# Pieces of an early key and value projection placed at the ends of two earlier stages of a decoder kernel

## The reference, cut to what matters

```python
x = layernorm(x + attention0(x))            # layer 0
x = layernorm(x + cross_attention0(x, ctx))
x3 = layernorm(x + quantised_ffn0(x))
xn = layernorm(x3)                          # layer 1
mx = silu(conv(xn, ema_kernel) + xn * omega)
x4 = layernorm(gated_attention(x3, xn, mx))
K = ctx @ Wk.T + bk                         # 16 heads of 64, L1_xattn
V = ctx @ Wv.T
...
out = mixture_of_experts(layernorm(x4 + cross_attention1(x4, K, V)))
```

## Time and profile before

| | |
|---|---|
| median of 3 runs | 2559.37 us (2551.48 to 2562.3) |
| profiled execution | 2562.5 us, span 2560.5 us |
| PE busy | 2319.6 us, 91% of the span |
| ACT, DVE, POOL busy | 45%, 53%, 33% |
| mean granted clock of TensorE | 0.962 of 2.4 GHz |
| the four stages end (first work of the next) at | 837.8, 982.5, 1144.8 us for l0_xattn, l0_ffn, mega_conv |

### The profile page before, as it was taken

One profiled execution on the slowest core, in us unless ns is written; L12 is line 12 of the kernel. 1 busy time (PEld: TensorE's weight loads), 2 busy tenths in 40 slices (PEclk: granted clock), 3 DMA queues, 4 the chain that ended last, 5 costly groups with the idle time before them and its releaser, 6 DMA issues. The chain is left out here.

```text
span 2560.5 us, 45165 instructions
## 1 busy us (share of the span) xinstructions
PE 2319.6 (91%) x17378; PEld 1806.3 (71%) x17378; DVE 1345.0 (53%) x2520; ACT 1147.0 (45%) x1965; POOL 844.7 (33%) x873
## 2 busy tenths in 40 slices
PE   6999998799997897989898969999998799999993
PEld 5677777466665565756565758888886688888893
DVE  5688888478877670003544446778877211111113
ACT  4567676356665563434323235555564111111113
POOL 4354554234444581000101023445544212121221
PEclk9899999799999898999999989999999899999997
DMA  3524544100110569362111022333332665666564
GB/s 108 127 76 123 138 128 118 56 28 26 51 50 26 192 225 267 133 213 90 51 49 50 14 110 83 121 116 100 104 98 96 257 194 175 196 175 196 170 222 143
DMA packets 212899, 313.25 MB, mean 122 GB/s; under 512 B 63824, under 2 KB 195536, under 8 KB 199376
## 3 DMA queue, kind: packets, MB, share of 16 engines
q1 hardware_dynamic: 190832, 255.25, 31.6%
q0 software_dynamic: 13440, 17.90, 3.9%
q10 hardware_dynamic: 8416, 37.23, 3.7%
HBM read 188.88 MB, written 121.45 MB: 121 GB/s over the span
## 5 line engine op out<-in xcount | busy, mean ns | idle before, releaser
L2773 ACT ACTIVATE dec_area<-me_ps_h 128x512 f32<-128x512 f32 (+1 forms) x160 | 88.7, 555 | 423.7 <-PE me_ps_h L2751 414.9
L2814 DVE TENSOR_SCALAR me_yo<-me_ps_y,moe_xg 128x256 f32<-128x256 f32 x72 | 34.8, 484 | 429.2 <-PE me_ps_y L2761 410.2
L2689 POOL DMA_INDIRECT xo<-me_yo,me_row x72 | 112.7, 1566 | 410.8 <-DVE me_yo L2814 357.3
L2751 PE MATMUL me_ps_h<-me_xt,me_w 128*128 128x256 f32 (+1 forms) x1056 | 210.0, 357 | 0.0
L2761 PE MATMUL me_ps_y<-me_w,dec_area 128*128 128x256 f32 x944 | 209.2, 379 | 0.7 <-DVE me_yo L2814 0.7
L2224 POOL TENSOR_TENSOR l1x_e<-l1x_e,l1x_ri 128x1024 f32<-128x1024 f32 x64 | 121.7, 1902 | 240.2 <-DVE l1x_ri L2484 240.2
L2761 PEld LDWEIGHTS me_ps_y<-me_w,dec_area 128*128 128x128 f32 x944 | 178.7, 190 | 25.1 <-issue 1.1
L2751 PEld LDWEIGHTS me_ps_h<-me_xt,me_w 128*128 128x128 f32 x1056 | 181.7, 190 | 20.2
L868 POOL TENSOR_TENSOR l0x_e<-l0x_e,l0x_ri 128x1024 f32<-128x1024 f32 x64 | 120.0, 1896 | 199.5 <-DVE l0x_ri L1088 199.5
L2323 PE MATMUL l1x_ps_p<-l1x_xct,dec_area 128*128 128x256 f32 x512 | 125.9, 391 | 0.7 <-ACT l1x_xct L2409 0.7
L2361 PE MATMUL l1x_ps_o<-dec_area,l1x_ot 128*128 128x256 f32 x512 | 120.4, 389 | 1.4 <-ACT l1x_ot L2432 1.4
(11 more groups left out here) (423 smaller groups left out, 5530.7 us busy)
## 6 DMA issues: line engine op xcount, KB each, us to landing
me_w<-in_w SPq DMA_DIRECT2D x33, 2048.0 KB, 9.4
xs<-dec_zero SPq DMA_DIRECT2D x31, 1032.0 KB, 6.8
k<-kv_kt ACTq DMA_DIRECT2D x16, 1024.0 KB, 4.2
v<-kv_va ACTq DMA_DIRECT2D x16, 1024.0 KB, 4.5
l1x_kt<-k SPq DMA_DIRECT2D x16, 1024.0 KB, 5.0
l1x_va<-v SPq DMA_DIRECT2D x16, 1024.0 KB
moe_w_first<-in_w SPq DMA_DIRECT2D x7, 2048.0 KB, 9.7
moe_xg<-xs SPq DMA_DIRECT2D x32, 258.0 KB, 2.9
```

The costliest lines, as they stand in the source:

```text
L2689: pool.indirect_dma_start(token_rows, bass.IndirectOffsetOnAxis(row[:, j % 2, q:q + 1], 0), yo[:, j % 2, q, :], None, compute_op=ALU.add). ...
L2751: last = pe.matmul(ps_h[i % HB][:, f % 2, 0:P * size(j)], weights(j)[:, FFN * c + f * P:FFN * c + f * P + P], xt[:, j % 2, c, 0:P * size(j ...
L2773: act.activation(h[:, j % 2, 2 * i:2 * i + 2, 0:P * size(j)], ps_h[i % HB][:, :, 0:P * size(j)], ACT.Gelu).then_inc(gelued, 1)
```

## The change

Pieces 0 to 4 move into `l0_xattn`, behind its last steps; 8 pieces more go behind the last step of `l0_ffn`; all piece numbers in `l0_ffn` and `mega_conv` shift accordingly, so that 27 instead of 40 are left behind the convolution. In `l0_xattn` the pieces use the two projection banks ps_p.

```diff
+L0X_LAST, FFN_FIRST, FFN_STEP, FFN_LAST = 5, 10, 7, 8
...
         ps_p = [kit.ps(f"ps_p{i}", [P, GP]) for i in range(2)]
+        kv.share_banks(ps_p)
...
+                def early(n):
+                    if n == 0:
+                        pe.wait_ge(v_biased, TILES)
+                    kv.make(pe, n, n + 1)
                 walk([(0, TILES, score), (2, TILES, transpose_e), at_part(0, transposes), at_part(1, project_q), at_part(2, project_k),
-                      at_part(3, project_v), (2, TILES, apply), (3, TILES, multiply)])
+                      at_part(3, project_v), (2, TILES, apply), (3, TILES, multiply), (TILES + 1, L0X_LAST, early)])
...
                 walk([(2, TILES, copy_et), at_part(0, copy_xct), at_part(1, bias_q), at_part(2, bias_k), (0, TILES, exponentials),
-                      (2, TILES, copy_ot), (8, TILES, normalise)])
+                      (2, TILES, copy_ot), (8, TILES, normalise), (TILES + 1, 2, lambda n: kv.keep(act, n, n + 1)),
+                      (TILES + 5, L0X_LAST - 2, lambda n: kv.keep(act, n + 2, n + 3))])
...
+    def share_banks(self, banks):
+
+        self.ps = banks
...
-FFN_FIRST, FFN_STEP = 10, 7
...
-                kv.keep(act, 0, 2)
+                kv.keep(act, L0X_LAST, L0X_LAST + 2)
                 sum_squares(0)
                 act.wait_ge(w_loaded, 5 * 16)
                 act.activation(w[:, :, :], w_i[:, :, :], ACT.Copy).then_inc(w_ready, 1)
-                kv.keep(act, 2, 5)
+                kv.keep(act, L0X_LAST + 2, L0X_LAST + 5)
                 sum_squares(1)
-                kv.keep(act, 5, FFN_FIRST)
+                kv.keep(act, L0X_LAST + 5, L0X_LAST + FFN_FIRST)
                 for s in range(1, NG + 2):
-                    first = FFN_FIRST + FFN_STEP * (s - 1)
+                    first = L0X_LAST + FFN_FIRST + FFN_STEP * (s - 1)
...
                     if 0 <= s - 1 < NG:
                         kv.keep(act, first + 1, first + FFN_STEP)
+                kv.keep(act, first, first + FFN_LAST)
...
-                kv.make(pe, 0, FFN_FIRST)
+                kv.make(pe, L0X_LAST, L0X_LAST + FFN_FIRST)
                 pe.wait_ge(w_ready, 1)
                 for s in range(NG):
-                    first = FFN_FIRST + FFN_STEP * s
+                    first = L0X_LAST + FFN_FIRST + FFN_STEP * s
                     transposes(s)
                     kv.make(pe, first, first + 1)
                     multiply(s)
                     kv.make(pe, first + 1, first + FFN_STEP)
+                kv.make(pe, first + FFN_STEP, first + FFN_STEP + FFN_LAST)
...
-        begin = FFN_FIRST + FFN_STEP * TILES // 4
+        begin = L0X_LAST + FFN_FIRST + FFN_STEP * TILES // 4 + FFN_LAST
         among = begin + CONV_FIRST
```

## The result

The changed kernel took 2545.79 us (median of 9 runs, 2541.2 to 2550.36), the kernel before 2562.3 beside it on the same chip (9 runs, 2551.48 to 2568.81). The ratio is 0.9931, 95% interval 0.9918 to 0.9943, which is 17.7 us less (14.6 to 21.0); the two medians lie 16.5 apart. The profiled executions differ by 18.3 us of span, 2560.5 against 2542.2 (2562.5 and 2543.89 us in all). On two further chips the same kernel gave 0.9912 (0.9883 to 0.9941) and 0.9948 (0.9929 to 0.9966).

What follows compares the result with a forecast made beforehand. PE and its pieces, not transfers, were taken to set the convolution stage's end. Terms -20.9 - 0.7 - 1.6 + 0.3 + 1.8 - 0.3 + 2.8 = -18.6 us gave 2541 us from a median of 2559.4; range 2534 to 2551.

Steps and rivals of the forecast that it cites:

- tail: End of the convolution stage: eleven full pieces and two transposes go, -20.9 us; attention starts 9 us behind mx's landing.
- lead (transpose, clock, xn): Ahead of the convolution: -0.75 us for one transpose more, -1.6 for the clock, +0.3 for the load of xn.
- end of cross attention: Last steps of cross attention: piece 0 free, two pairs of copies delay the last normalisation, +1.8 us, bounds 1.7 to 6.4.
- feed-forward's front: Feed-forward's start: held by the load of constants, early pieces save nothing; +0.75 us less 0.25 for a shorter copy.
- its steps: The feed-forward's eight steps: seven transposes instead of six, -0.75 us, from -3 to +7 around this.
- drain: End of the feed-forward: eight pieces behind the last step start the next stage later, +2.8 us, bounds +1 to +5.
- the first rival: Convolution stage: transfers bind, xn lands 5 us past its bound and mx 10 late; 2548 us, chance 0.12.
- The clock's 1.6: Convolution stage's opening: PE pauses under 2 us instead of 13.4, so full clock returns; 0 to 1.6 us, 1.6 taken.
- The 0.3 taken for it: Ahead of the convolution: cost of xn landing later beside up to one more 1 MB store, from 0 to 1.5 us.
- the 1.5 of the upper bound: Ahead of the convolution: full cost if the extra store shares the DMA engines with xn's load; sum 1.2 us poorer.
- The second rival: Feed-forward's steps: ACT's order stretches them as other pieces stand beside squares and normalisations; +7 us, 2548, chance 0.09.
- The third: Both drains and into the convolution's lead: moved pieces run at 1.2 GHz, 1.72 us more each; 2558 to 2596, chance 0.05.

Runs made afterwards that it cites:

- drain_twelve: The change with twelve instead of eight pieces in the feed-forward's drain: 2550.48 us, ratio 0.9934 to the kernel before.
- drain_four: The change with four instead of eight pieces in the feed-forward's drain: 2554.32 us, ratio 0.9955 to the kernel before.
- store_held: The change with the store of group 0's keys issued behind ACT's weight copy: 2547.11 us, ratio 0.9931 to the kernel before.
- change_again: The change itself, unaltered, run once more on another chip: 2545.81 us, ratio 0.9912 to the kernel before.
- front_four: The change with ACT copying four pieces instead of two before it waits for the feed-forward's constants: 2547.23 us, ratio 0.9936 to the kernel before.
- front_four_held: front_four with the store of group 0's keys also issued behind ACT's weight copy: 2539.52 us, ratio 0.9905 to the kernel before.
- eight_from_28: The change with eight instead of five pieces in cross attention, from step 28 on: 2547.36 us, ratio 0.9919 to the kernel before.

## Why the prediction was right, and where it was not

The forecast, 2541 us, was 18.4 below the stated median; 17.7 were measured by the ratio, and 2545.8 us lies in the range. The time itself lies 4.8 above the forecast, 2.9 of it because the kernel before had a median of 2562.3 beside the change and not 2559.37. Step by step, in us, from the three traces of the change:

| step | predicted | measured |
|---|---|---|
| tail | -20.9 | -20.8 |
| lead (transpose, clock, xn) | -2.0 | -2.7 |
| end of cross attention | +1.8 | +1.4 |
| feed-forward's front | +0.5 | +4.5, +2.1, +4.3 |
| its steps | -0.75 | -0.8 |
| drain | +2.8 | +2.7 |
| outside these stages | 0 | -2.6 in the first pair |

- **Tail.** Eleven pieces at 1.72 and two transposes at 0.97 came out as worked out, one for one. The last part of mx was issued at 1114.8 and landed 4.1 us later, 9.4 ahead of attention: the first rival (transfers bind) had no part in it. drain_twelve's tail of 43.98 still scales by the piece.
- **Lead.** The clock's 1.6 came back: PE paused 1.50 us and the stage opened at full clock; drain_four shows what happens otherwise. xn landed earlier than in the bounds, not later: its last part was issued at 999.8 and landed 21.4 us after, 31.6 behind the stage's start (33.0 before, bounds 33.0 to 37.2). The 0.3 taken for it was not due, and neither was the 1.5 of the upper bound. The Trainium skill (DMA: Bandwidth & Descriptors, "Queues, rings and completion order") has each DMA engine take turns between the queues that have work. The measured lead doesn't settle whether it does so here, as the extra store was issued 3.0 us before the load (986.61 and 989.61). Nor does the feed-forward's start: the constants on SP's queue landed 8.7 us after their issue and the 1 MB store on ACT's 12.4 after its own, but the constants had been issued 1.2 us earlier. The lead came out 0.4 below the two terms for transpose and clock; that is not explained.
- **End of cross attention.** The mechanism was as described (piece 0 free, two pairs of copies between normalisations). The path grew by 1.4 us, less than the two pairs' 1.7, which the prediction had as its lower bound.
- **Drain.** PE, copies and the 0.7 us to the next stage came as in the sum. "Every further us on PE or ACT there costs in full" is nearly what drain_twelve shows: 6.3 us in the drain for four pieces of 6.9.
- **The step that failed: "Its start is held by the load of constants ... the early pieces save nothing here", +0.5 for the front.** It took the constants' landing as fixed, and the clock behind the wait as full. Neither holds. In the three traces of the change the landing came 1.3 to 2.1 us later, about 1 us of it probably with the new store of keys (store_held). And with two banks PE's fifth piece waits for ACT, which waits for the constants. Before, the four pieces ahead of that were a transpose piece and three key pieces, most of it at the lower clock, and took 10.3 us (837.8 to 848.1), until the wait was over; after, they take 7.8 (838.7 to 846.4). The 3.6 to 4.3 us that PE then stands are no cost by themselves, as the fifth piece waited for the same event before; but in two traces of three the clock was lower behind them, which is the other 1.4 to 1.6 us. The 4.5 of the first trace is 2.1 for the landing, 1.6 for the clock and 0.8 for the rest, where the prediction had 0.5; the 2.1 of change_again is 1.3 and 0.8. That the stand could be removed, and was worth more than the term itself, the prediction did not see: front_four and front_four_held took the stand away, and front and steps fell by 3.2 to 6.8 us.
- **The second rival**, ACT's order in the steps, did not come: 97.70 in all traces, as predicted. **The third**, moved pieces at 1.2 GHz, came in a small form where it was not looked for, at the feed-forward's front.
- In the first pair the front was 3.9 us worse than in the sum, lead, end and the rest together 1.1 better, and 2.6 came from stages that the change does not touch. The total of -18.3 against -18.6 is therefore closer than its terms, by luck; the repeats put these stages at -15.7, -18.1 and -15.9.

What stays open: what share of the later landing is the store's (eight_from_28 has 8.0 us without it), when a pause lowers the clock and when not, and what makes the untouched stages move by 6 us and more between executions.

## What to carry to other kernels

Work moved into an idle stretch is free only up to the event that ends the stretch, and that event is to be found first: here four pieces were free in the drain, the next four cost 40% of their price, four more nearly all of it. Where work crosses into the next stage's start, ask how far ahead of its consumer the producer may run: where the consumer stands at a wait, a producer with two buffers stands too as soon as it arrives early, and that is mended by letting the consumer empty the buffers before it waits. Gaps inside a chain of dependent steps were no cover here for blocks longer than the gap.

## What the runs showed of the hardware

- TensorE's clock after pauses, in this kernel. Inside the front of the kernels with five pieces in cross attention, pauses of 2.52 to 3.71 us behind four pieces were followed by products at full clock, those of 4.29 and 4.31 us by slower ones for some 8 us. That is no border between the two: in eight_from_28 a pause of 3.32 us behind four pieces brought a granted clock of 0.77 and then 0.61 over 5.3 us, and two key pieces took 5.41 us instead of 3.62:

```profile
850.72 5.41 PE L1266 MATMUL ffn_ps_kv<-kv_ct,kv_w_kv 128*128 128x256 f32 x16 [3.32 <-ACT kv_kt L1303]
```

  Between two stages of pieces, 1.50 us kept the full clock and 5.56 brought 0.50, that is 1.2 GHz. At the feed-forward's start, behind five pieces in an otherwise light stage, 3.6 us brought the lower level in every trace of the change (two pieces 5.1 us). In cross attention 2.38 us did before the change, while the same pause in the trace of front_four was followed by the full clock (16 transposes in 1.09 + 1.09 us), and in store_held the clock fell only after the next pause, of 0.76 us. The length of the pause alone doesn't tell it. The granted clock of the changed kernel's front:

```profile
838.40:842.00 3.60, 3.34 (x5) 1.58 (x6) 0.00 (x0) 0.00 (x0) 3.56 (x1) 0.57 0.57 148
...
846.00:850.00 4.00, 0.41 (x1) 0.00 (x0) 0.42 (x2) 0.85 (x3) 0.00 (x0) 1.00 0.75 277
850.00:854.00 4.00, 3.29 (x6) 1.70 (x7) 2.78 (x3) 1.60 (x4) 2.78 (x2) 0.72 1.00 380
854.00:858.00 4.00, 4.00 (x16) 3.16 (x16) 3.83 (x12) 3.02 (x12) 0.54 (x1) 0.85 0.45 164
```

- The same 128 KB constant landed 5.7 to 8.7 us after its issue across thirteen traces of this start; the means with and without the 1 MB store on the other queue lie 1.2 us apart.
